# TensorE posts one semaphore increment for two groups in four edge passes of a graph network

## Time and profile before

| what | value |
|---|---|
| median of 3 runs | 10192.11 us (10191.21 to 10203.29) |
| the profiled execution's own time | 10213.39 us |
| its span | 10211.6 us |
| TensorE matmul (PE) busy | 5172.9 us, 51% |
| VectorE (DVE) busy | 5157.6 us, 51% |
| ScalarE (ACT) busy | 2350.8 us, 23% |
| GpSimd (POOL) busy | 6159.7 us, 60% |
| share of the 16 DMA engines: POOL's queue q0, and q1 | 20.4%, 9.4% |
| mean granted TensorE clock | 0.673 of full speed |

### The profile page before, as it was taken

The page is one execution under the profiler, slowest core; times in us unless marked ns, Lnnn a source line. Parts: engine busy times, 40 slices in busy tenths (PEclk is TensorE's granted clock), DMA queues, the critical chain, the costliest instruction groups (busy, mean ns, idle before and its releaser), DMA issues. The chain is left out here.

```text
span 10211.6 us, 117807 instructions
## 1 busy us (share of the span) xinstructions
PE 5172.9 (51%) x26943; PEld 4434.7 (43%) x27385; DVE 5157.6 (51%) x11737; ACT 2350.8 (23%) x7991; POOL 6159.7 (60%) x6684
## 2 busy tenths in 40 slices
PE   1544444447365666666673323333345565666655
PEld 1434433435254555555552222222244555555553
DVE  4644544546466666666652222222245555555556
ACT  1212211224244444444460000000021111111114
POOL 5666666662566555555516666666656666666664
PEclk9556556667677777777786656555576766666677
DMA  4222222222444444444421111111123333333331
GB/s 110 46 46 47 46 46 46 47 46 86 100 101 99 99 98 98 98 98 98 99 68 47 46 47 46 47 46 46 46 62 109 100 101 101 102 100 102 101 100 43
DMA packets 869663, 769.76 MB, mean 75 GB/s; under 512 B 385028, under 2 KB 727929, under 8 KB 868606
## 3 DMA queue, kind: packets, MB, share of 16 engines
q0 software_dynamic: 230416, 528.66, 20.4%
q1 hardware_dynamic: 626235, 228.48, 9.4%
q10 hardware_dynamic: 12344, 5.06, 0.2%
HBM read 707.24 MB, written 54.30 MB: 75 GB/s over the span
## 5 line engine op out<-in xcount | busy, mean ns | idle before, releaser
L1007 POOL DMA_INDIRECT rows_h<-t_d,idx x1563 | 1482.3, 948 | 1024.9 <-issue 396.3
L581 POOL DMA_INDIRECT rows_sum<-t_d,idx x1563 | 1474.7, 944 | 962.8 <-issue 453.5
L581 POOL DMA_INDIRECT rows_mlp<-t_d,idx x1548 | 1468.7, 949 | 834.1 <-remote 419.0
L1007 POOL DMA_INDIRECT rows<-t_d,idx x1477 | 1396.7, 946 | 812.6 <-issue 409.7
L1152 PEld LDWEIGHTS pn_h<-S_h,rows_h 128*128 128x128 f32 x6252 | 1098.1, 260 | 258.5 <-issue 223.2
L1152 PE MATMUL pn_h<-S_h,rows_h 128*128 128x128 f32 x6252 | 1141.6, 348 | 124.8 <-issue 110.3
L1047 ACT ACTIVATE rows_h<-rows_h,wc_h 128x64 f32<-128x64 f32 x4688 | 1135.9, 334 | 17.1 <-issue 7.0
L772 DVE TENSOR_TENSOR big<-big,pn_sum 128x512 f32 x391 | 269.2, 689 | 1687.0 <-remote 1535.6
L620 PE MATMUL pre_mlp<-dw_mlp,ST_mlp 128*128 128x128 f32 x3126 | 674.5, 379 | 475.8 <-DVE ST_mlp L59 185.3
L627 PE MATMUL pn_sum<-zb_sum 128*128 128x512 bf16 x325 | 175.4, 540 | 1294.4 <-DVE big L772 1089.9
L620 PEld LDWEIGHTS pre_mlp<-dw_mlp,ST_mlp 128*128 128x128 f32 x3126 | 591.2, 280 | 528.5 <-issue 513.8
(11 more groups left out here) (361 smaller groups left out, 8634.5 us busy)
## 6 DMA issues: line engine op xcount, KB each, us to landing
dw_mlp<-bd_d SPq DMA_DIRECT2D x1563, 64.0 KB
frow_mlp<-t_d ACTq DMA_DIRECT2D x1920, 0.5 KB
frow_h<-t_d SPq DMA_DIRECT2D x1792, 0.5 KB
lrb_h<-lrrow_d SPq DMA_DIRECT2D x196, 128.0 KB
lrb_mlp<-lrrow_d SPq DMA_DIRECT2D x98, 256.0 KB
rows_h<-t_d,idx POOLq DMA_INDIRECT x1563
dw_h<-xp_d SPq DMA_DIRECT2D x1563, 3.0 KB
rows_sum<-t_d,idx POOLq DMA_INDIRECT x1563
```

Of the source, the lines that this page charges most:

```text
L581: e.indirect_dma_start(rows[:, g % NR, j, :], None, table, bass.IndirectOffsetOnAxis(ap=idx[:, b, t:t + 1].bitcast(I32), axis=0)).then_inc ...
L1007: e.indirect_dma_start(rows[:, g % NR, j, :], None, table, bass.IndirectOffsetOnAxis(ap=idx[:, b16, t:t + 1].bitcast(I32), axis=0)).then_i ...
```

## The change

Four places where TensorE increments a semaphore once per group now do so once per two groups: on the last matmul of each odd group, by 2, and for the last group (g = 390, an even one) by 1. These are `expand` and `place` of `edge_light` (the latter serves the third and the fourth pass, the former only the fourth), and `expand` (second pass) and `tally` (first pass) of `edge_soft`. The placing of the first two passes (L1155) keeps its increment per group. No wait, no order of instructions, no buffer and no other engine's stream is altered; the totals that the semaphores reach are the same.

```diff
@@ -618,7 +618,8 @@
                 e.wait_ge(s_st, g + 1)
                 for j in range(SIZE[g]):
                     last = e.matmul(pre[g % 2][:, j, :], ST[:, g % 2, j, :], dw[:, g % ND, j, :], start=True, stop=True)
-                last.then_inc(s_ex, 1)
+                if g % 2 or g == GR - 1:
+                    last.then_inc(s_ex, g % 2 + 1)
 
             def place(g, r0):
 
@@ -639,7 +640,8 @@
                         x = frow[n][:, k % DEEP, :]
                     last = e.matmul(pn[g % 2][:, bass.ds(r0[j], P)], x, S[:, g % NS, j, :],
                                     start=False, stop=(j == SIZE[g] - 1))
-                last.then_inc(s_mm, 1)
+                if g % 2 or g == GR - 1:
+                    last.then_inc(s_mm, g % 2 + 1)
 
             lag = 1 if mlp else 0
             if mlp:
@@ -1159,7 +1162,8 @@
                 e.wait_ge(s_ho, g + 1)
                 for j in range(SIZE[g]):
                     last = e.matmul(hist[:, :], ho[:, g % 2, j, :], lo[:, g % 2, j, :], start=False, stop=False)
-                last.then_inc(s_hm, 1)
+                if g % 2 or g == GR - 1:
+                    last.then_inc(s_hm, g % 2 + 1)
 
             def number():
```

## The result

| | kernel before | kernel changed |
|---|---|---|
| median of 3 runs | 10192.11 us | 10390.58 us (10378.30 to 10422.42) |
| ratio, 95% interval | | 1.019 [1.0167, 1.0212] |
| span of the profiled execution | 10211.6 us | 10388.8 us |

A forecast was written before the change was run, and what follows sets the result against it. The prediction held that TensorE's increments arrive late while POOL issues gathers, forcing POOL to pause. Its terms, -95 + 0 - 10 + 0 = -105 us, gave 10108 us profiled, 10087 us median; forecast's own range 10010 to 10165, overall 9900 to 10290.

The forecast's parts named there:

- No change: Rival, 0.16: the pause pays 0.135 us for every gather, so the increments' number hardly matters; 10175 to 10210 us.
- Third pass, -95 us: Increments carrying pairs let more groups through between POOL's pauses; middle taken between gains of 30 and 159 us.
- The end of -159 us: Third pass, best case: openings go on every 10.6 us, the pace of a pair, giving 2072 us.
- one increment gets through per 10.6 us, whatever it is worth: Claimed rate at which TensorE's increments pass while POOL runs, read from adds at 10.86 and 21.43 us.
- the warning in the earlier trace: Fourth pass's opening: DVE sat 18.28 us before the finish, so openings don't always go on.
- Fourth pass, 0: Both of a pair's increments are held and POOL restarts at 11.9 us as today; ends -195 and +20 us.
- First pass, -10: Fewer queued increments may lengthen some cycles from 8 to 12 gathers; -10 us, ends 0 and -60.
- Second pass, 0 with ends -40 and +100: Fewer increments ahead of the chain's, against DVE's spread waiting for a younger expansion every odd iteration; 0 us.
- The signs named for this pass: Second pass: more DVE idle time before L1449 (the spread), less before L1463 (the add).
- The slower one: Rival, 0.22: a pair's increment misses the time after restart, third pass falls to 8-gather cycles; +96 us, 10288 us.
- The bigger gain: Rival, 0.20: with fewer increments, place's passes before POOL must pause in the fourth pass too; 9892 us.
- its rule: Forecast range 10010 to 10165 us: both ends of the third pass, half those of the others; forecast's chance 0.42.

The follow-up runs named there:

- the unpaced runs: Third pass: POOL no longer waits for TensorE, which multiplies a constant; on the kernel before 10642.73 us, on the changed kernel (increments in pairs) 10832.90 us.
- the run without gathers: Third pass: POOL issues only the first eight groups' gathers and all later groups reuse those rows, against the kernel before; 8604.24 us.

## Why the prediction was wrong

**What bounds the kernel.** Right in its core, on chips of the first kind: increments of TensorE are late while POOL gathers, and on time without gathers. Wrong in one step: "POOL's gathers start 1.25 us apart when nothing holds them". They do for a while; over a pass a gather costs 1.383 us on these chips even with no wait at all. The third pass's floor is 2161 us (on two chips), not 1950, and its 2222 us stand 61 us above it. That was the "No change" rival's sentence, that the pause pays 0.135 us for every gather, whoever waits. A second reading was wrong too: POOL is not the busiest engine in every pass. In the second, have DVE at 1592.86 of 2506 us, 64%, and POOL at 59%; the wait that the change adds is one of DVE.

**Third pass, -95 us; measured +1 (and +4 on another chip).** Two steps failed. The end of -159 us (2072 us) was below the floor, and so was the middle that I took (2136). And "one increment gets through per 10.6 us, whatever it is worth" is refuted by the unpaced runs: 25.2 us for one group, 50.4 us for a pair. Within a cycle, too, a pair takes what two single groups took: four groups are through at 15.1 us after the restart, between the 10.86 and 21.43 us at which the third and the fourth came before. The third pair was to pass at 21.4 us after the restart; it was ready at 20.3 and passed at 34. I had the warning in the earlier trace rows and averaged it with the earlier trace rows instead of asking what an opening counts.

**Fourth pass, 0; measured -2 between the profiled executions, but +9 by its own gathers on each of two other chips (2282 us with the pairs and 2273 without on the one, 2283 and 2274 on the other).** Right, within the end of +20 given for a pair that ends late. **First pass, -10; measured +4 and -2.** Nothing, as near as can be told.

**Second pass, 0 with ends -40 and +100; measured +172.** This is the step that made the result. The prediction named the place: every odd iteration the spread waits for an expansion one group younger, in front of the add and the chain. It priced that wait by the length of the spread, 0.68 us, and capped it by DVE's idle time before its adds. Both are wrong in kind. What a wait costs is how late its increment comes, and the same text had just shown an increment 11 us late in the third pass and DVE held for 18.28 us in the fourth. The spread's wait came to 479.6 us in place of at most 100. The cap failed because idle time there is no store that the wait draws on: in the wait shown above the chain's step behind it is late, so TensorE's placing is, so POOL's ring is, and POOL stands where it had run. The spread had no such wait before (17.8 us in all) only because two buffers gave it one iteration of distance; the pair took exactly that. The signs named for this pass did come: idle time before the spread went from 69.6 to 601.7 us, that before the add from 211.9 to 75.6 (375 of its 391 adds are in the trace).

**The rivals.** The slower one, at 0.22, had the right sign and the wrong pass: it let the third pass fall from cycles of 24 gathers to 8, and 63 of its 64 cycles stayed at 24. The bigger gain has no support: the fourth pass keeps its pauses. "No change" described nearly all that happened outside the second pass.

**The range.** The 10010 to 10165 of the forecast is not what its rule gives. Both ends of the third pass and half those of the others add up, from the median before, to 9886 to 10222. The measured 10391 is outside that as well.

**Increments and ends of matmuls.** The Trainium skill's 26 ns per increment ("TensorE: Matmul & The Clock Gate", section "The cost: per-tile semaphore tail") would make the 975 increments worth an estimated 25 us. With pairs and no added wait, 195 fewer increments gave 1.0003 [0.9993, 1.0012]; 26 ns each would be 5 us, below what that shows, and the other four series, removed together, lost 13 us (1 to 25) where by that rule they were to win an estimated 20. TensorE sets none of these lengths, so no run here shows the 26 ns themselves.

The Trainium skill, "Perfetto Trace Analysis", section "Summary: the profiler window per engine type", calls a matmul's end an estimate. This case's traces bear the ends out at this size: the run without gathers has 388 adds with no wait above 0.8 us, and all its updates of `s_mm` 0.01 us behind the recorded ends, so the lateness is no error of them.

## What to carry to other kernels

Merging increments moves every waiter to the youngest of the merged group; before doing it, list the waiters, see what stands behind each on its engine, and price the wait by the lateness that the trace shows for that semaphore's engine, not by the work that is delayed. If a waiter's distance is one buffer, give it another first: here that turned the loss into next to nothing (on one chip, ratio 1.0016 with all pairs and the buffer, 1.0188 with the one pair and no buffer). And a rate read between stalls isn't an engine's rate: take the stall's cause away once and see what the whole stretch then costs.

## What the runs showed of the hardware that was not expected

- While POOL issues indirect DMAs without a pause, on chips of the first kind, TensorE's increment reaches VectorE once per 18 gathers, 25.2 us, 22 us after the matmul's end; a pair needs 50.4 us.
- The gathers themselves then cost 1.383 us on average, on two chips, in a repeating pattern of records of 0.95, 1.09 and 1.79 us; with POOL's pauses the third pass comes to 1.42 us.
- Chips differ in this. On three chips the kernel before takes 10104 to 10220 us (and 10192 in the first result), on two it takes 8520 and 8532 us, 16% less, with gathers 1.250 us apart and increments on time. What sets a chip's kind wasn't found; each was used in one sitting only, so a lasting property of the chip and its state at that time are not told apart. A change that trades increments or waits has to be measured on both kinds.
- Every experiment's execution here has a recorded span and clock, so no run shows whether the recording itself takes a part in the delay. A hint that it might: in the third pass the kernel before has 355 of its 391 updates of `s_mm` in the trace, and the run without gathers and those on the second kind of chip have all 391 (in the second pass some are missing on both kinds).
